# New slots for the side work of a two-stage attention kernel, and its second copy of the keys on ScalarE

## Chip, cores and metric

One NeuronCore of a Trainium2 chip runs the whole program. The metric is the time of one execution in microseconds (us), measured on the device; less is better. The kernel before takes 1200.07 us (median of 3 runs, 1199.62 to 1205.99).

## What is computed

The input is 16 images of 32 x 32 positions with 64 channels, float32. Cut to what matters, the reference is:

```python
# stage 1: group norm, then full attention over the 1024 positions of an image
h = group_norm(x, gn_scale, gn_bias, num_groups=16)
q, k, v = h @ wq + bq, h @ wk + bk, h @ wv + bv
w = softmax(q @ k.T * 64 ** -0.5)
t = x + (w @ v) @ wo + bo
# stage 2: layer norm over channels, then causal attention
n = layernorm(t)
q, k, v = n @ Wq.T, n @ Wk.T, n @ Wv.T
t = t + softmax(causal(q @ k.T / 8)) @ v
# stage 3: every one of 32 experts picks the top 8 positions of each image
u = layernorm(t)
p = softmax_over_positions(u @ gate_w.T + gate_b)
vals, idx = top_k(p, 8)                    # per image and expert
pooled = sum_k(vals * u[idx])              # one vector per image and expert
out = t + scatter_add(idx, vals * (gelu(pooled @ w1) @ w2))
```

## The kernel before

**The pipeline.** The attention part handles one image per iteration, 17 iterations in all (`emit(i)`; the first four and the last three written out, ten in a loop of two). Each iteration has two phases. Phase 1 of iteration i computes the scores and values of stage 1 for image i; phase 2 those of stage 2 for image i - 1. A phase is a list of units (`UNITS`): 16 units of 128 keys by 512 queries in phase 1, and 15 of 128 to 512 queries in phase 2, where the causal mask leaves some out. For each unit TensorE makes a score tile with two matmuls (`score`, L739 and L741: operands are split in a high and a low part, so two matmuls stand for one; the first also adds the row of negated maxima), ScalarE takes its exponential (`exponentials`, L883) into `probs`, and once for two key tiles TensorE multiplies with the values (`values`, L759; four groups per phase, the last of them run in the next phase). There are three score banks, so TensorE is at most three units ahead of ScalarE.

**Maxima first.** The exponential needs the maximum of each query's scores beforehand. So, one phase ahead, "pieces" compute the scores a first time (`piece`, L720), VectorE reduces each to a maximum (L1121), with two banks in turn (`NM` is 2). When the last piece is reduced, step `r1` or `r2` negates the maxima (L1111), transposes them on TensorE (L702), copies them out (L1116), and SP moves them by DMA (`move_row`, L584) into one row of `queries_lo`. The first score of the next phase waits for that DMA (`row_loaded`).

**Side work.** Everything else of an image is cut into named steps, each of which runs on several engines in turn: `p1.st`, `p1.g1`, `p1.g2`, `p1.g3`, `p1.w` (group norm statistics and the scaled weights), `p1.qa`, `p1.qb`, `p1.ka`, `p1.kb` (projections of queries and keys, two halves each: TensorE `mm`, ScalarE writes the high part `hi`, VectorE the low part `lo`), `xp` (splits the next input into high and low part), `f1.rs`, `f1.out`, `f2.out` (row sums and output projections), `l1a`, `l1b`, `l2a`, `l2b`, `l2c` (layer norms), `p2.tr`, `p2.qa`, `p2.qb` (transposition and projection for stage 2), `moe.tr`, `moe.lg` (gate logits), `r1`, `r2`. The steps of one chain (`proj_step`, `fin_step`, `norm_step`) count on one semaphore, so each waits for all before it in its chain.

**What sets the order.** Nothing is planned at run time. Each engine runs through the slots of a phase, two for each unit (32 in phase 1, 30 in phase 2). On TensorE an even slot begins with a score, then come value groups (`VALUE_SLOTS`; the last entry is a slot of the following phase), pieces (`PIECE_SLOTS`) and side steps (`AT["pe"]`). ScalarE does the exponential of the unit in its even slots, then `copy_out` (`COPY_SLOT`), then its side steps; VectorE its pieces, then its side steps; GpSimd the sums of the probabilities of stage 1 for the denominators (`add_rows`, L967 and L970, at `ADD_SLOTS`; the last in phase 2), the bias (`add_bias`, L977, at `BIAS_SLOT`), then its side steps. A slot is only a place in the order of one engine: an engine that has nothing to wait for goes on. The engines meet through semaphores. Steps in one slot follow the order of `SIDES_1` and `SIDES_2`. `AT_FIRST` replaces some entries in phase 1 of the first iteration.

**The second copy of the keys.** Stage 1 needs the high part of the keys twice: in `keys[1]` (its upper 64 partitions then receive the low part) and, with a row of ones, in `keys_hi`. The kernel before writes the first by ScalarE (L835) and has SP copy it to `keys_hi` by DMA (`copy_keys`, L576) once the low part of `p1.kb` is written. SP's order in an iteration is: load the transposed input of image i + 2 (`next_xt`), store image i - 2 (`store`), `copy_keys(i + 1)`, row 2 (`move_row(2, i - 1)`), load x of image i + 2 (`next_x`), row 1 (`move_row(1, i + 1)`). SP waits in this order too.

Of the kernel before, what the change touches and what calls it, by code (L numbers as in the profile page):

```python
# [18 lines left out]
HALF = S // 2  # L19
# [38 lines left out]
def sides_of(ph, first):  # L58
# [4 lines left out]
AT = {  # L63
# [9 lines left out]
}  # L73
AT_FIRST = {
    "pe": {"p1.g1": 1, "p1.g2": 2, "p1.w": 4},
    "act": {"p1.g1": 1, "p1.w": 4},
    "dve": {"p1.st": 0, "p1.g1": 1, "p1.g2": 2, "p1.g3": 3, "p1.w": 4},
    "pool": {"p1.g2": 2},
}

PIECE_SLOTS = {
    1: [1, 3, 5, 7, 9, 11, 12, 13, 14, 15, 16, 17, 19, 21, 23],
    2: [2, 3, 4, 6, 7, 8, 9, 10, 11, 12, 14, 16, 17, 19, 20, 22],
}
VALUE_SLOTS = {1: [9, 17, 25, 1], 2: [9, 17, 24, 1]}
ADD_SLOTS = [None, 4, 8, 12, 16, 20, 24, 1]
COPY_SLOT = {1: 2, 2: 2}
BIAS_SLOT = 6

# [83 lines left out]
def count_increments():  # L173
# [22 lines left out]
    inc("row_loaded1", ("row", 0), 16)  # L196
    inc("keys_copied", ("keys", 0), 16)
    for i in range(0, B + 1):
        for ph in (1, 2):
# [24 lines left out]
            if ph == 1 and i + 1 < B:  # L224
                inc("keys_copied", ("keys", i + 1), 16)
            if ph == 1 and 0 <= i - 2:
# [146 lines left out]
def attention_part(nc, ctx, g):  # L373
# [153 lines left out]
    def _(sp):  # L527
# [43 lines left out]

        def copy_keys(n):

            ready = held(done("proj_step", "p1.kb", n, "lo"))
            sp.wait_ge(proj_step, ready)
            sp.dma_start(keys_hi[n.parity][0:C, :].bitcast(F32), keys[1][n.parity][0:C, :].bitcast(F32)).then_inc(  # L576
                keys_copied, 16)

        def move_row(s, n):
# [15 lines left out]

        next_xt(Image(1))
        copy_keys(Image(0))
        move_row(1, Image(0))

        def emit(i):  # L600
            for k in range(IN_MAIN):
                if i.trip is None and (i.first == B - 1 and k < 2 or i.first == B and k == 2):
                    load_logits(k)
            if i.first + 2 < B:
                next_xt(i + 2)
            if i.first >= 2:
                store(i + (-2))
            if i.first + 1 < B:
                copy_keys(i + 1)
            if i.first >= 1:  # L610
                move_row(2, i + (-1))
            if i.first + 2 < B:
                next_x(i + 2)
            if i.first + 1 < B:
                move_row(1, i + 1)
# [195 lines left out]
    def _(act):  # L811
        def side(name, n):
# [18 lines left out]
            elif name in ("p1.qa", "p1.qb", "p1.ka", "p1.kb"):  # L831
# [3 lines left out]
                nc.scalar.activation(dst[:, a * HALF:(a + 1) * HALF], proj_ps[:, :], ACT.Identity,  # L835
                                     bias=qk_bias[q][:, b:b + 1], scale=1.0).then_inc(proj_step, 1)
            elif name == "p2.tr":
                act.wait_ge(proj_step, done("proj_step", name, n, "tr"))
# [540 lines left out]
```

## Time and profile before

| | before |
|---|---|
| median of 3 runs | 1200.07 us (1199.62 to 1205.99) |
| the profiled execution's own time | 1198.53 us |
| its span, first to last instruction | 1196.8 us |
| TensorE busy (matmuls) | 920.4 us, 77% of the span |
| VectorE busy | 586.5 us, 49% |
| ScalarE busy | 464.6 us, 39% |
| GpSimd busy | 418.9 us, 35% |
| mean granted TensorE clock | 0.845 |
| DMA, all queues | 47.53 MB, 40 GB/s over the span |

The busy time of an engine is the time in which an instruction of it runs. The granted clock is the share of full speed that TensorE was given; it has two levels, 1.2 and 2.4 GHz, so a mean of 0.5 is the lower level throughout. The attention part runs from about 50 to 1127 us; what follows is the expert part, which the change does not touch. In the rows further down, `[2.63 <-DMA queries_lo<-rows]` behind an instruction means that its engine stood idle 2.63 us before it and that the DMA named ended this.

### The profile page before, as it was taken

The numbers are of one execution on the slowest core, as the hardware profiler recorded it, in microseconds if no ns is written. First come the engines' busy times: TensorE is split into PE (matmuls) and PEld (weight loads), VectorE is DVE, ScalarE is ACT, GpSimd is POOL, SyncE is SP. The second block draws the span as 40 slices with busy tenths as digits, with TensorE's granted clock in tenths as the row PEclk, the third lists the DMA queues.
The fourth block names the chain that finished last, engine by engine and source line by source line (L and its number), as shares of the span: only waits on it lengthen the run. The fifth ranks groups of instructions, "written<-read, shape, count | busy, mean of one in ns | idle before, by whom it ended". The sixth has DMA issues, their size and how long they took to land. (4 is left out here: it accounts for less than half of the span.)

```text
span 1196.8 us, 14532 instructions
## 1 busy us (share of the span) xinstructions
PE 920.4 (77%) x4278; PEld 527.1 (44%) x4278; DVE 586.5 (49%) x1663; ACT 464.6 (39%) x952; POOL 418.9 (35%) x246
## 2 busy tenths in 40 slices
PE   2777888787888787887878887878878788866546
PEld 1334454534444453535444454545453444434326
DVE  3544554445564554544455544545454545544124
ACT  2222444353535343443435343434435353442320
POOL 1162524262616244242626152442426261610000
PEclk9985978798898888797988888897879888876758
DMA  4010011020201111010202011111102011000089
GB/s 89 11 43 27 18 27 36 5 58 9 58 10 45 23 27 40 27 40 1 57 9 57 9 45 22 26 40 27 31 9 57 9 31 36 23 18 23 18 177 268
DMA packets 67368, 47.53 MB, mean 40 GB/s; under 512 B 36047, under 2 KB 56815, under 8 KB 67311
## 3 DMA queue, kind: packets, MB, share of 16 engines
q1 hardware_dynamic: 67311, 46.90, 16.2%
q8 instruction: 20, 0.33, 0.1%
q14 instruction: 37, 0.30, 0.1%
HBM read 27.88 MB, written 10.49 MB: 32 GB/s over the span
## 5 line engine op out<-in xcount | busy, mean ns | idle before, releaser
L883 ACT ACTIVATE probs<-scores 128x512 f32<-128x512 f32 (+3 forms) x496 | 252.8, 514 | 455.9 <-PE scores L741 450.2
L1121 DVE TENSOR_REDUCE maxima<-maxima_in 128x1 f32<-128x512 f32 (+3 forms) x496 | 276.8, 581 | 271.9 <-PE maxima_in L720 268.0
L970 POOL TENSOR_TENSOR prob_sum<-prob_sum,probs 128x1024 f32<-128x1024 f32 x96 | 227.0, 2365 | 58.4 <-ACT probs L883 54.5
L720 PE MATMUL maxima_in<-keys,queries 128*128 128x512 f32 (+3 forms) x496 | 210.4, 453 | 27.8 <-DVE maxima L1121 27.3
L741 PE MATMUL scores<-queries,keys 128*128 128x512 f32 (+3 forms) x496 | 196.6, 397 | 0.0
L720 PEld LDWEIGHTS maxima_in<-keys,queries 128*128 128x128 f32 x496 | 108.7, 220 | 105.4 <-DVE maxima L1121 72.0
L739 PE MATMUL scores<-queries_lo,keys_hi 65*128 65x512 f32 x256 | 128.4, 502 | 34.2 <-DMA queries_lo<-rows 31.4
L759 PE MATMUL values_out<-probs,x_sb 128*64 128x512 f32 x512 | 144.7, 692 | 1.0 <-ACT probs L883 1.0
L937 POOL TENSOR_TENSOR ln<-ln,minus_half 128x8 f32<-128x8 f32 x32 | 52.8, 1649 | 251.5 <-DVE ln L1106 251.5
L947 POOL TENSOR_TENSOR x_stack<-x_twice,x_stack 64x1024 fp32r<-64x1024 f32 x16 | 37.4, 2339 | 229.9 <-ACT x_stack L819 229.9
L741 PEld LDWEIGHTS scores<-queries,keys 128*128 128x128 f32 x496 | 108.4, 218 | 8.2 <-issue 3.4
L739 PE MATMUL scores<-queries_lo,keys 128*128 128x384 f32 (+3 forms) x240 | 100.8, 420 | 0.0
L759 PE MATMUL values_out<-probs,normed 128*64 128x128 f32 (+3 forms) x480 | 99.5, 507 | 0.7 <-ACT probs L883 0.6
L967 POOL TENSOR_TENSOR prob_sum<-probs 128x1024 f32<-128x1024 f32 x16 | 37.8, 2364 | 150.0 <-ACT probs L883 119.4
L739 PEld LDWEIGHTS scores<-queries_lo,keys_hi 65*128 65x128 f32 x256 | 55.8, 218 | 58.0 <-issue 33.2
L739 PEld LDWEIGHTS scores<-queries_lo,keys 128*128 128x128 f32 x240 | 52.2, 217 | 36.0 <-issue 21.9
L759 PEld LDWEIGHTS values_out<-probs,x_sb 128*64 128x64 f32 x512 | 35.3, 155 | 72.5 <-issue 68.1
L737 PE MATMUL scores<-mask_k,ident_b 128*128 128x128 bf16 x128 | 31.8, 249 | 39.6 <-DMA queries_lo<-rows 39.6
L759 PEld LDWEIGHTS values_out<-probs,normed 128*64 128x64 f32 x480 | 34.6, 158 | 41.9 <-issue 37.2
L852 ACT ACTIVATE u_sb<-t,ln 128x64 f32<-128x64 f32 x128 | 45.5, 434 | 14.9 <-POOL ln L940 14.9
L737 PEld LDWEIGHTS scores<-mask_k,ident_b 128*128 128x128 bf16 x128 | 16.4, 128 | 54.5 <-DMA queries_lo<-rows 30.6
L719 PE MATMUL maxima_in<-mask_q,ident_b 128*128 128x128 bf16 x128 | 32.2, 252 | 7.5 <-DVE maxima L1121 6.7
(174 smaller groups left out, 1107.6 us busy)
## 6 DMA issues: line engine op xcount, KB each, us to landing
x_twice<-in_x_t SPq DMA_DIRECT2D x32, 256.0 KB, 4.1
x_halves<-in_x_t SPq DMA_DIRECT2D x16, 256.0 KB, 2.7
x_sb<-in_x SPq DMA_DIRECT2D x16, 256.0 KB, 3.0
keys_hi<-keys SPq DMA_DIRECT2D x16, 256.0 KB, 3.0
u_all<-u_sb SPq DMA_DIRECT2D x16, 256.0 KB, 2.6
t_scratch<-t SPq DMA_DIRECT2D x16, 256.0 KB, 3.0
total<-t_scratch SPq DMA_DIRECT2D x16, 256.0 KB, 4.9
w_sb<-in_w SPq DMA_DIRECT2D x1, 2080.0 KB
```

Source lines behind the costliest of these rows:

```text
L720: pe.matmul(maxima_in[:, p % NM, 0:w * P], queries[s][q][:, c * P:(c + 1) * P], keys[s][q][:, h * HALF:h * HALF + w * P], start=not diagon ...
L737: pe.matmul(bank[:, 0:P], ident_b[:, :], mask_k[:, :], start=True, stop=True)
L739: pe.matmul(bank, low[:, key_cols(t)], queries_lo[s][q][:, lo:hi], start=not diagonal, stop=False, skip_group_check=diagonal)
L741: pe.matmul(bank, keys[s][q][:, key_cols(t)], queries[s][q][:, lo:hi], start=False, stop=True, skip_group_check=diagonal).then_inc(scores_ ...
L759: mm = pe.matmul(values_out[a * C:(a + 1) * C, j0 * P:HALF], v_sb[:, t, :], probs[:, t % NP, lo:hi], start=t == 0, stop=t == NT - 1, skip_ ...
L852: ins = nc.scalar.activation(u_sb[:, t, :], t2[:, t, :], ACT.Identity, bias=ln[:, 2, t:t + 1], scale=ln[:, 1, t:t + 1])
L883: nc.scalar.activation(probs[:, t % NP, lo:hi], scores[:, (u + (s - 1) * len(UNITS_1)) % NST, 0:hi - lo], ACT.Exp, scale=SCALE).then_inc(e ...
L937: nc.gpsimd.tensor_tensor(ln[:, 1, :], ln[:, 0, :], minus_half[:, :], ALU.pow).then_inc(norm_step, 1)
L947: nc.gpsimd.tensor_tensor(x_stack[C:P, :], x_twice[C:P, :], x_stack[C:P, :], ALU.subtract).then_inc(split_step, 1)
L967: nc.gpsimd.tensor_tensor(prob_sum[:, :], probs[:, 0, :], new, ALU.add).then_inc(rows_added, 2)
L970: nc.gpsimd.tensor_tensor(prob_sum[:, :], prob_sum[:, :], new, ALU.add).then_inc(rows_added, 1)
L1121: V.reduce_max(maxima[s][:, c, h:h + 1], maxima_in[:, p % NM, 0:w * P], AX.X).then_inc(maxima_taken, 1)
```

## The change

All slot tables get new values, for TensorE (`pe`), ScalarE (`act`), VectorE (`dve`) and GpSimd (`pool`). `AT_FIRST` gets entries that hold the projections of the first iteration at their former slots. The DMA `copy_keys` and its wait leave SP's queue. In its place, ScalarE, after writing a half of the keys (`p1.ka`, `p1.kb`), waits for that write and copies the half from `keys[1]` to `keys_hi`; the semaphore `keys_copied` now counts 2 for an image instead of 16, and the first score of phase 1 waits for it as before.

```diff
 AT = {
-    "pe": {"f2.out": 2, "p1.qa": 6, "p1.qb": 11, "p1.ka": 16, "p1.kb": 22, "moe.tr": 24, "moe.lg": 26, "r2": 29,
-           "f1.rs": 3, "f1.out": 5, "p1.g1": 7, "p1.g2": 9, "p1.w": 12, "p2.tr": 15, "p2.qa": 19, "p2.qb": 22,
-           "r1": 26},
-    "act": {"p1.qa": 7, "p1.qb": 12, "l2b": 14, "p1.ka": 17, "l2c": 18, "p1.kb": 23, "moe.tr": 25, "moe.lg": 27,
-            "p1.g1": 8, "p1.w": 13, "p2.tr": 15, "p2.qa": 19, "p2.qb": 22, "xp": 24},
-    "dve": {"f2.out": 2, "l2a": 4, "p1.qa": 8, "p1.qb": 13, "p1.ka": 18, "p1.kb": 24, "r2": 28,
-            "p1.st": 1, "f1.rs": 3, "f1.out": 5, "l1a": 6, "p1.g1": 7, "p1.g2": 9, "p1.g3": 11, "p1.w": 13,
-            "p2.tr": 16, "p2.qa": 20, "p2.qb": 23, "r1": 25},
-    "pool": {"l2a": 6, "l1a": 7, "l1b": 8, "p1.g2": 10, "xp": 25},
+    "pe": {"f1.rs": 2, "f1.out": 4, "p1.g1": 1, "p1.g2": 3, "p1.w": 9, "p2.tr": 20, "p2.qa": 27, "p2.qb": 29,
+           "r1": 26, "p1.qa": 6, "p1.qb": 14, "p1.ka": 16, "p1.kb": 22, "r2": 27, "f2.out": 6, "moe.tr": 23,
+           "moe.lg": 24},
+    "act": {"p1.g1": 0, "p1.w": 9, "p2.tr": 20, "p2.qa": 27, "p2.qb": 29, "xp": 22, "p1.qa": 6, "p1.qb": 12,
+            "p1.ka": 16, "p1.kb": 18, "l2b": 17, "l2c": 17, "moe.tr": 18, "moe.lg": 23},
+    "dve": {"p1.st": 0, "f1.rs": 3, "f1.out": 9, "l1a": 9, "p1.g1": 1, "p1.g2": 3, "p1.g3": 6, "p1.w": 10,
+            "p2.tr": 21, "p2.qa": 22, "p2.qb": 29, "r1": 21, "p1.qa": 7, "p1.qb": 14, "p1.ka": 20, "p1.kb": 26,
+            "r2": 29, "f2.out": 0, "l2a": 8},
+    "pool": {"l1a": 20, "l1b": 29, "p1.g2": 11, "xp": 29, "l2a": 17},
 }
 AT_FIRST = {
-    "pe": {"p1.g1": 1, "p1.g2": 2, "p1.w": 4},
-    "act": {"p1.g1": 1, "p1.w": 4},
-    "dve": {"p1.st": 0, "p1.g1": 1, "p1.g2": 2, "p1.g3": 3, "p1.w": 4},
+    "pe": {"p1.g1": 1, "p1.g2": 2, "p1.w": 4, "p1.qa": 6, "p1.qb": 11, "p1.ka": 16, "p1.kb": 22},
+    "act": {"p1.g1": 1, "p1.w": 4, "p1.qa": 7, "p1.qb": 12, "p1.ka": 17, "p1.kb": 23},
+    "dve": {"p1.st": 0, "p1.g1": 1, "p1.g2": 2, "p1.g3": 3, "p1.w": 4, "p1.qa": 8, "p1.qb": 13, "p1.ka": 18,
+            "p1.kb": 24},
     "pool": {"p1.g2": 2},
 }
 PIECE_SLOTS = {
-    1: [1, 3, 5, 7, 9, 11, 12, 13, 14, 15, 16, 17, 19, 21, 23],
-    2: [2, 3, 4, 6, 7, 8, 9, 10, 11, 12, 14, 16, 17, 19, 20, 22],
+    1: [7, 7, 11, 15, 17, 17, 18, 19, 21, 21, 23, 23, 24, 24, 26],
+    2: [0, 0, 1, 2, 4, 11, 13, 14, 15, 17, 17, 18, 19, 20, 21, 21],
 }
-VALUE_SLOTS = {1: [9, 17, 25, 1], 2: [9, 17, 24, 1]}
-ADD_SLOTS = [None, 4, 8, 12, 16, 20, 24, 1]
-COPY_SLOT = {1: 2, 2: 2}
-BIAS_SLOT = 6
+VALUE_SLOTS = {1: [15, 27, 28, 1], 2: [10, 22, 29, 0]}
+ADD_SLOTS = [None, 10, 21, 22, 25, 27, 29, 11]
+COPY_SLOT = {1: 0, 2: 1}
+BIAS_SLOT = 12
...
-    inc("keys_copied", ("keys", 0), 16)
+    inc("keys_copied", ("keys", 0), 2)
...
-                inc("keys_copied", ("keys", i + 1), 16)
+                inc("keys_copied", ("keys", i + 1), 2)
...
-        def copy_keys(n):
-
-            ready = held(done("proj_step", "p1.kb", n, "lo"))
-            sp.wait_ge(proj_step, ready)
-            sp.dma_start(keys_hi[n.parity][0:C, :].bitcast(F32), keys[1][n.parity][0:C, :].bitcast(F32)).then_inc(
-                keys_copied, 16)
-
...
-        copy_keys(Image(0))
...
-            if i.first + 1 < B:
-                copy_keys(i + 1)
...
                 nc.scalar.activation(dst[:, a * HALF:(a + 1) * HALF], proj_ps[:, :], ACT.Identity,
                                      bias=qk_bias[q][:, b:b + 1], scale=1.0).then_inc(proj_step, 1)
+                if b:
+
+                    act.wait_ge(proj_step, done("proj_step", name, n, "hi"))
+                    nc.scalar.copy(keys_hi[q][0:C, a * HALF:(a + 1) * HALF],
+                                   keys[1][q][0:C, a * HALF:(a + 1) * HALF]).then_inc(keys_copied, 1)
```

## Rows read from the trace of the kernel before

**Rows 1.** The table by stretch, middle of the run: us, busy (count) per engine, clock, DMA.

```profile
core 0: us, PE busy (x) PEld busy (x) DVE busy (x) ACT busy (x) POOL busy (x), PEclk, DMA share, GB/s
108.22:1044.40 936.18, 761.95 (x3306) 432.42 (x3306) 481.65 (x1397) 397.15 (x810) 379.53 (x216) 0.86 0.12 30
165.35:1014.09 848.74, 688.16 (x2994) 391.11 (x2994) 438.53 (x1277) 359.53 (x737) 336.93 (x193) 0.86 0.12 30
```

**Rows 2.** The same table inside one image (625.25 to 691.60 us), same columns.

```profile
627.40:634.60 7.20, 6.08 (x20) 5.02 (x21) 3.79 (x24) 2.95 (x5) 0.78 (x1) 0.54 0.00 0
...
656.78:662.20 5.42, 5.42 (x13) 1.83 (x14) 0.00 (x0) 0.60 (x1) 0.50 (x1) 0.50 0.00 0
...
670.00:675.30 5.30, 2.57 (x11) 1.55 (x10) 3.99 (x12) 1.17 (x3) 4.22 (x4) 1.00 0.09 21
675.30:683.00 7.70, 7.27 (x27) 4.31 (x28) 3.93 (x8) 3.32 (x7) 0.00 (x0) 0.56 0.00 0
683.00:691.60 8.60, 5.32 (x33) 3.65 (x34) 4.31 (x8) 3.77 (x9) 2.34 (x1) 1.00 0.01 1
```

**Rows 3.** The waits of TensorE, 165.35 to 1014.09 us: total, times, longest.

```profile
PE scores L737 <- DMA queries_lo<-rows: 33.9, 13, 2.9
PE scores L739 <- DMA queries_lo<-rows: 29.2, 14, 2.4
PE proj_ps L644 <- DVE affine L1030: 20.0, 12, 1.7
...
PE fin_ps L702 <- DVE neg_max L1111: 15.7, 13, 1.3
PE fin_ps L688 <- ACT out_raw L891: 15.4, 13, 1.3
```

**Rows 4.** The timeline: start, duration, engine; a values group, a score, half of `l2b`/`l2c`.

```profile
642.14 1.94 PE L759 MATMUL values_out<-probs,x_sb 128*64 128x512 f32 x8
...
644.29 0.39 PE L739 MATMUL scores<-queries_lo,keys_hi 65*128 65x512 f32 x1
...
644.52 0.39 PE L741 MATMUL scores<-queries,keys 128*128 128x512 f32 x1
...
645.44 1.42 ACT L852 ACTIVATE u_sb<-t,ln 128x64 f32<-128x64 f32 x4
```

**Rows 5.** The timeline at the ends of both phases: SP's DMAs and the first scores.

```profile
623.39 0.69 SPq L584 DMA_DIRECT2D queries_lo<-rows  x1
625.25 0.50 PE L739 MATMUL scores<-queries_lo,keys_hi 65*128 65x512 f32 x1 [1.92 <-DMA queries_lo<-rows]
...
653.56 0.54 SPq L576 DMA_DIRECT2D keys_hi<-keys  x1
...
654.20 0.70 SPq L584 DMA_DIRECT2D queries_lo<-rows  x1
...
656.78 0.29 PE L737 MATMUL scores<-mask_k,ident_b 128*128 128x128 bf16 x1 [2.63 <-DMA queries_lo<-rows]
```

**Rows 6.** Groups by line and shape, whole run: busy us, mean ns of one.

```profile
L970 POOL TENSOR_TENSOR prob_sum<-prob_sum,probs 128x1024 f32<-128x1024 f32 x96 | 227.0, 2365 | 58.4 <-ACT probs L883 54.5
L1121 DVE TENSOR_REDUCE maxima<-maxima_in 128x1 f32<-128x512 f32 x304 | 202.5, 684 | 155.2 <-PE maxima_in L720 152.1
L883 ACT ACTIVATE probs<-scores 128x512 f32<-128x512 f32 x304 | 179.2, 596 | 376.9 <-PE scores L741 373.4 <-POOL prob_sum L970 2.5
...
L840 ACT CAST keys<-proj_ps 64x512 fp32r<-64x512 f32 x16 | 9.3, 579 | 0.0
```

**Rows 7.** The timeline of `f2.out` and `l2a` on VectorE, and GpSimd's first add.

```profile
630.66 0.18 DVE L1077 RECIPROCAL recip<-fin_ps 128x4 f32<-128x4 f32 x1 [3.50 <-PE values_out L688]
...
631.95 0.68 DVE L1093 TENSOR_TENSOR t<-t 128x512 f32<-128x512 f32 x1
...
633.83 2.36 POOL L967 TENSOR_TENSOR prob_sum<-probs 128x1024 f32<-128x1024 f32 x1 [8.43 <-ACT probs L883]
...
634.49 1.72 DVE L1105 TENSOR_SCALAR ln<-ln_mv 128x8 f32<-128x8 f32 x1
...
636.13 0.16 DVE L1106 TENSOR_SCALAR ln<-ln_mv 128x8 f32<-128x8 f32 x1
```

## The prediction

> **What bounds the kernel now.** No engine does. I read first the table by stretch. An image takes 848.74 / 13 = 65.3 us in the middle of the run [rows 1]; in that time TensorE is busy 688.16 / 13 = 52.9 us, VectorE 33.7, ScalarE 27.7 and GpSimd 25.9, at a granted clock of 0.86. TensorE is nearest to a bound, but it waits, and runs slowly after waiting. The same table inside one image shows that [rows 2]: three stretches of 7.20, 5.42 and 7.70 us stand at clocks of 0.54, 0.50 and 0.56, that is mostly at the lower level (1.2 GHz), and ahead of two of them stands a thin stretch, TensorE busy 2.57 of 5.30 us and 5.32 of 8.60; ahead of the third stands a wait for a DMA. Then I read who holds TensorE up [rows 3]: the two rows of maxima that come back by DMA before each phase's first score (33.9 / 13 = 2.61 us and 29.2 / 14 = 2.09 us), the `affine` column (1.67), `neg_max` (1.21) and `out_raw` (1.18). So each phase ends in a chain (maxima, `neg_max`, transpose, row, DMA) with nothing left to do beside it, and its start is paid twice: the wait, and then the low clock. The change is worth what it puts beside these waits.
>
> **What it gives, per image.**
> - *Row 2 (end of phase 1).* `r2` goes from TensorE slot 29 to 27 and now has score 14, values group 2 and score 15 behind it. A score is two matmuls 0.23 us apart, 0.46; a group of eight takes 1.94 [rows 4]. That is 2.9 us. The row needs 2.57 us from issue to its first user [rows 5], plus the cast on VectorE, some 0.3. The wait goes; next late would be exp 13, long done. `neg_max` is covered by group 1 (1.94), which stands ahead of `r2` in slot 27. Gain 2.61 + 1.21, and the stretch at 0.50 behind it, 5.42 x 0.5 = 2.71: **6.5**.
> - *Row 1 (end of phase 2).* `r1` stays at TensorE slot 26, but the two `p2.q` projections move behind it (27, 29), with score 14 and group 2: about 2.9 us with their own wait, against 1.86 for the row [rows 5]. `f2.out` moves from slot 2 to 6, two scores later, so that the copy of `out_raw` which it waits for is done. Gain 2.09 + 1.18, and 6.08 us of work at 0.54 (x 0.46 = 2.80): **6.1**.
> - *Group statistics.* `p1.g1` and `p1.g2` move to slots 1 and 3, and GpSimd's `p1.g2` now stands ahead of `l1a` and `l1b`, not behind them; `p1.w` at slot 9 should find `affine` ready. Gain 1.67 + 7.70 x 0.44 = 3.39: **5.1**.
>
> Together 17.7 us.
>
> **What comes back, per image.**
> - *The copy of the keys.* The DMA (16 of 256 KB) leaves SP. In the old order it was issued at 653.56, just ahead of row 2 at 654.20, which took 0.7 us longer than row 1 [rows 5]; with row 2 hidden that is worth 0. SP's wait for `p1.kb` ahead of row 2 goes too; it would have ended before the row's cast (VectorE slots 26 and 29): 0. ScalarE gets two 64x512 copies. No row has this copy from SBUF; the nearest, 64x512 from PSUM, takes 0.58 [rows 6], and I take that, plus 0.1 for the wait on its own last result (ends: 0 if ScalarE has time to spare, 1.4 if all is on the path). From slot 16 on ScalarE then has in a row `p1.ka`, the first copy, `l2b` and `l2c` (2 x 1.42 [rows 4]), exp 9, `moe.tr`, `p1.kb`, the second copy and exp 10, which score 13 waits for. With 0.60 for each exp and each activation of 128x512 that is 7.2 us. TensorE's way from slot 16 to 26 is about 6.0, set by VectorE's ten reduces of 128 to 512 columns and `p1.ka`'s `lo`. So score 13 waits **1.2**; with a DMA it would not, so this part of the change speaks against it.
> - *`p1.ka`* waits for `p1.qb`'s `lo`, which VectorE does behind all of `l2a`. From `f2.out`: its scaling with one piece 1.3 and `l2a` 4.3 less 1.55 [rows 7], two `lo` of about 0.75 and two more small pieces, together 6.4 us, while TensorE has 5.8 of work; with the hops **0.8** (0 to 2.4). The 1.55: `nm` (L1105) took 1.72 us and ended when GpSimd's add (633.83 to 636.19) did; its twin L1106 took 0.16 just behind. In the new order GpSimd should be done with add 1 and the bias by then and wait for `l2a` itself, so I take 0.17.
> - *`r1`* waits behind `p2.tr` on VectorE (slot 21: piece 15 and two subtractions of as many columns, 0.68 each, `neg_max` and hops, 2.6) while TensorE has 1.8 us: **0.8** (0 to 1.5).
> - *The clock.* Rows 2 show low stretches behind thin ones. The new order still has one: eleven pieces in phase 2 that VectorE paces at 0.68 us each [rows 6]. I leave one stretch of the three, **3.0** (0 to 9).
>
> Costing nothing: `f1.rs`, `f1.out`, `l1a`, the bias and the other side work change place on engines that wait anyway (GpSimd is idle 39 of 65 us [rows 1]); VectorE, standing at slot 0 for `f2.out`, has no piece before slot 7, where the first now comes. The first image keeps its projection slots. If GpSimd's slack goes, the price is the second case below.
>
> A page bears on `l2a`. The Trainium skill (SBUF — State Buffer, § Who interferes with whom) says that a VectorE instruction with two SBUF inputs, not only one in a two-port mode, is shut out for a whole GpSimd instruction that reads SBUF. By it the add that opens `l2a`, which may now fall beside GpSimd's bias, would be up to 0.9 us late, and the time 13 us more. No run here shows that case; in the old order this add had an idle GpSimd beside it.
>
> **The sum.** 17.7 - 5.8 = 11.9 us per image. The order repeats from 108.22 to 1044.40 us, 936.18 / 65.3 = 14.3 images [rows 1]; I count nothing for the ends. 14.3 x 11.9 = 170 us. From the profiled execution's own 1198.5 us (its span is 1196.8) that leaves 1028.5; the median of the runs lies 1.5 above that execution, so **1030 us**, an image at 53.4.
>
> **The rivals.**
> - *As forecast* (70%): from 965 (of what comes back only the copy's wait stays: 16.5 x 14.3 = 236) to about 1080.
> - *GpSimd's adds and the clock take half of it* (20%). `l2a` now stands ahead of adds 2 to 7, six of 2.37 us [rows 6], and `f1.rs` waits for the last, with VectorE's pieces from the fifth on queued behind it. By my count the last add ends 3.0 us into phase 2 and TensorE asks for it at 4.2: 1.2 us to spare. If it is 4 us late, 2.8 is lost, and with a second low stretch (3.0) 6.1 us per image is left: 87 us, 1113. For: the adds are packed behind exps 9 to 15, which come late. Against: GpSimd's sum.
> - *The gains come back as new waits* (4%): row 2 lands after score 15 all the same and the low clock stays; 1200. The copy alone may well show nothing, its DMA being hidden.
> - *Slower, by the clock* (6%). If stretches that VectorE paces are thin everywhere, TensorE may hold its lower level for most of the image. Its work at full level is 52.9 x 0.86 = 45.5 us; its idle time, 12.4, becomes 12.4 - 8.8 + 2.8 = 6.4 by the terms above. It turns slower where the mean granted clock of the middle falls under 45.5 / 58.9 = 0.77. At 0.75 an image takes 67.1 us: 1225. Against: the waits ahead of the low stretches are shorter or gone.
>
> The range holds the forecast and the second case: **965 to 1115 us**. Faster by over 0.5% (about what a measurement of this kernel can tell from no change) 90%, within 4%, slower 6%.
>
> **What would show it.** Right: waits for `queries_lo<-rows` under 0.5 us each, no clock near 0.5 at the start of either phase, L1105 near 0.17 us, an image of 52 to 56 us, score 13 and `p1.ka` waiting about 1 us, no `keys_hi<-keys` DMA and two ScalarE copies of about 0.6. Wrong: waits of `f1.rs` on `prob_sum` of some us (the second case), a mean clock under 0.8 (the last), or a wait I have not named of over 2 us per image.

## The result, and the profile after

The changed kernel takes **924.47 us** (median of 4 runs, 921.86 to 927.96), the kernel before, run beside it on the same chip, 1202.93. The ratio is 0.7687, with a 95% interval of 0.7647 to 0.7728: 278 us faster. The profiled execution took 927.96 us, with a span of 926.1. The forecast was 1030 us with a range of 965 to 1115, so the direction was right and the gain was larger than the range allowed.

The table by stretch of the changed kernel answers [rows 1] (the middle, the same 13 images) and [rows 2] (one image, here its two phases apart). Its columns: the stretch and its length, busy time of the engines, TensorE's granted clock, DMA share, GB/s. The last row is the thin stretch of eleven pieces in phase 2.

```profile
143.51:757.18 613.67, 594.49 (x2994) 334.18 (x2993) 422.08 (x1277) 372.27 (x763) 347.20 (x193) 1.00 0.14 35
...
380.17:403.96 23.79, 23.00 (x110) 12.62 (x108) 13.95 (x46) 17.38 (x34) 17.20 (x9) 1.00 0.24 61
403.96:427.47 23.51, 22.88 (x124) 13.04 (x123) 18.59 (x53) 11.35 (x25) 9.74 (x7) 1.00 0.05 12
...
415.50:423.00 7.50, 7.08 (x34) 4.16 (x35) 7.35 (x14) 3.79 (x9) 3.50 (x3) 1.00 0.00 1
```

An image takes 613.67 / 13 = 47.2 us, and 65.3 before: 18.1 less. TensorE's busy time per image goes from 52.9 to 594.49 / 13 = 45.7 us with the same work in it, and its idle time from 12.4 to 1.5. The first difference, 7.2, is the clock (0.86 before, 1.00 now), the second, 10.9, is waits. Of the 270.7 us by which the span is shorter, 235.1 lie in these 13 images (848.74 - 613.67); 21.8 lie ahead of them (165.35 - 143.51) and 13.8 behind.

Who holds TensorE up in the middle, first in the kernel before, whose five largest rows are [rows 3]; these are rows that the prediction did not use:

```profile
PE maxima_in L720 <- DVE maxima L1121: 17.7, 34, 0.9
...
PE proj_ps L630 <- DVE queries_lo L1059: 11.8, 13, 0.9
PE fin_ps L678 <- DVE recip L1065: 6.8, 13, 0.6
PE proj_ps L625 <- DVE bias_full L1041: 5.3, 12, 1.0
PE maxima_in L719 <- DVE maxima L1121: 5.0, 13, 0.4
```

The same view of the changed kernel, in full; score 13's two matmuls are L731 and L733 here (L739 and L741 before), the pieces L712 (L720 before):

```profile
PE scores L731 <- ACT probs L880: 6.2, 13, 0.5
PE fin_ps L617 <- ACT u_sb L849: 2.7, 13, 0.3
PE scores L731 <- DMA queries_lo<-rows: 0.3, 1, 0.3
```

All that is left is 9.2 us in 13 images, and before it was 160.8 (the ten largest rows). The waits for the row DMAs (but one of 0.3), `affine`, `neg_max`, `out_raw` and the pieces are gone. Of what was expected to come back, score 13's wait is there, 0.48 us an image on the matmul; on the weight loads the same wait stands larger:

```profile
PEld scores L731 <- ACT probs L880: 17.4, 14, 1.4
...
PEld fin_ps L694 <- DVE neg_max L1108: 13.8, 26, 0.8
```

The timeline of the changed kernel in one image answers [rows 5] and [rows 7]: `f2.out`/`l2a` on VectorE, the first of the two copies on ScalarE, score 13, row 2 and the first score of phase 2.

```profile
386.07 0.76 DVE L1090 TENSOR_TENSOR t<-t 128x512 f32<-128x512 f32 x1
386.24 1.73 POOL L974 TENSOR_TENSOR x_bias<-x_sb,bias_full 128x512 f32<-128x512 f32 x1
...
388.69 0.17 DVE L1102 TENSOR_SCALAR ln<-ln_mv 128x8 f32<-128x8 f32 x1
...
391.32 0.62 ACT L832 CAST keys_hi<-keys 64x512 fp32r<-64x512 f32 x1
...
397.73 0.50 PE L731 MATMUL scores<-queries_lo,keys_hi 65*128 65x512 f32 x1 [0.47 <-ACT probs L880]
...
401.45 0.72 SPq L579 DMA_DIRECT2D queries_lo<-rows  x1
401.51 1.94 PE L751 MATMUL values_out<-probs,x_sb 128*64 128x512 f32 x8
...
403.96 0.23 PE L729 MATMUL scores<-mask_k,ident_b 128*128 128x128 bf16 x1
```

Row 2 is issued at 401.45 and its first user starts at 403.96, 2.51 us later, as far apart as the 2.58 in [rows 5]; but values group 2 and score 15 now fill the time, and no wait is marked. `nm` (L1102) takes 0.17 us, where it took 1.72 in [rows 7].

### The profile page after: what moved, and what is told of

Read it like the earlier page. It is cut to its first block and busy times, and to the rows that moved or that the text cites. A ratio compares the mean times of both kernels' runs of the same rounds, so it can differ in the third digit from the quotient of the medians.

```text
span 926.1 us, 14558 instructions
## 1 busy us (share of the span) xinstructions
PE 815.0 (88%) x4278; PEld 467.7 (50%) x4278; DVE 569.6 (61%) x1663; ACT 479.5 (52%) x984; POOL 431.0 (47%) x246
## 5 line engine op out<-in xcount | busy, mean ns | idle before, releaser
L880 ACT ACTIVATE probs<-scores 128x512 f32<-128x512 f32 (+3 forms) x496 | 241.3, 512 | 208.9 <-PE scores L733 182.3
L712 PE MATMUL maxima_in<-keys,queries 128*128 128x512 f32 (+3 forms) x496 | 199.2, 434 | 17.3 <-DVE maxima L1118 9.0
L733 PE MATMUL scores<-queries,keys 128*128 128x512 f32 (+3 forms) x496 | 179.9, 365 | 0.0
L712 PEld LDWEIGHTS maxima_in<-keys,queries 128*128 128x128 f32 x496 | 94.6, 198 | 87.7 <-DVE maxima L1118 66.0
L751 PE MATMUL values_out<-probs,x_sb 128*64 128x512 f32 x512 | 124.0, 605 | 0.3 <-ACT probs L880 0.2
L731 PE MATMUL scores<-queries_lo,keys_hi 65*128 65x512 f32 x256 | 114.9, 449 | 9.4 <-ACT probs L880 6.4
L733 PEld LDWEIGHTS scores<-queries,keys 128*128 128x128 f32 x496 | 97.0, 196 | 6.7 <-issue 0.2
L731 PE MATMUL scores<-queries_lo,keys 128*128 128x384 f32 (+3 forms) x240 | 88.6, 373 | 0.0
L751 PE MATMUL values_out<-probs,normed 128*64 128x128 f32 (+3 forms) x480 | 83.7, 439 | 0.0
L964 POOL TENSOR_TENSOR prob_sum<-probs 128x1024 f32<-128x1024 f32 x16 | 38.3, 2392 | 81.5 <-PE values_out L680 54.6
L731 PEld LDWEIGHTS scores<-queries_lo,keys_hi 65*128 65x128 f32 x256 | 50.1, 196 | 46.1 <-issue 20.1
L731 PEld LDWEIGHTS scores<-queries_lo,keys 128*128 128x128 f32 x240 | 47.5, 198 | 2.1 <-issue 1.2
L1056 DVE TENSOR_TENSOR queries_lo<-proj_ps,queries 128x512 fp32r<-128x512 f32 x32 | 22.1, 692 | 42.1 <-ACT queries L842 42.1
L842 ACT CAST queries<-proj_ps 128x512 fp32r<-128x512 f32 x32 | 18.8, 587 | 38.0 <-PE proj_ps L623 38.0
L622 PE MATMUL proj_ps<-x_stack,w_lo 128*128 128x512 f32 x64 | 31.8, 497 | 7.5 <-DVE keys L1047 3.6
```

The source lines that it names most:

```text
L622: pe.matmul(proj_ps[:, :], lo, src[:, a * HALF:(a + 1) * HALF], start=True, stop=False)
L712: pe.matmul(maxima_in[:, p % NM, 0:w * P], queries[s][q][:, c * P:(c + 1) * P], keys[s][q][:, h * HALF:h * HALF + w * P], start=not diagon ...
L731: pe.matmul(bank, low[:, key_cols(t)], queries_lo[s][q][:, lo:hi], start=not diagonal, stop=False, skip_group_check=diagonal)
L733: pe.matmul(bank, keys[s][q][:, key_cols(t)], queries[s][q][:, lo:hi], start=False, stop=True, skip_group_check=diagonal).then_inc(scores_ ...
L751: mm = pe.matmul(values_out[a * C:(a + 1) * C, j0 * P:HALF], v_sb[:, t, :], probs[:, t % NP, lo:hi], start=t == 0, stop=t == NT - 1, skip_ ...
L880: nc.scalar.activation(probs[:, t % NP, lo:hi], scores[:, (u + (s - 1) * len(UNITS_1)) % NST, 0:hi - lo], ACT.Exp, scale=SCALE).then_inc(e ...
```

## The experiments

Two theories stood after the result. **The sum**: the gain is the sum of the places that the prediction named (row 2, row 1, group statistics), each worth its wait and the low clock behind it, whatever stands around it. **The whole**: the places depend on each other; a wait that is taken away at one place comes back at another unless the whole order fits, and the lesser moves, the pieces' slots above all, carry much of the gain. Four sets were run, each set's kernels on one chip beside the kernel before (1202.91, 1202.18, 1201.53, 1199.99 us). What an expectation calls A and B is what it says of them itself.

**The changed kernel again**, as the base of the first set.

> The changed kernel again, as the measure for the others of this set: 0.769 of the kernel before, about 924 us.

Measured 924.1 us (922.13 to 928.14), ratio 0.7687 (0.766 to 0.7715).

**The new slots with the old DMA copy.**

```diff
-                if b:
-                    act.wait_ge(proj_step, done("proj_step", name, n, "hi"))
-                    nc.scalar.copy(keys_hi[q][0:C, a * HALF:(a + 1) * HALF],
...
+        def copy_keys(n):
+            ready = held(done("proj_step", "p1.kb", n, "lo"))
+            sp.wait_ge(proj_step, ready)
+            sp.dma_start(keys_hi[n.parity][0:C, :].bitcast(F32), keys[1][n.parity][0:C, :].bitcast(F32)).then_inc(
...
             if i.first >= 2:
                 store(i + (-2))
+            if i.first + 1 < B:
+                copy_keys(i + 1)
```

> The new slots, with the second copy of the keys by SP's DMA as before. Theory A (TensorE is the bound now: an image takes 47.2 us of which it is busy 45.7, and it waits for the exponential of score 13 only 0.5 us): at most 0.5 x 14 = 7 us less than the changed kernel, and no more than 10 us more, since row 2 then leaves SP behind 256 KB and its 2.5 us of cover are just used up. Theory B (the prediction: the copies hold up score 13 by 1.2 us per image): 17 us less, about 907.

Measured **911.45 us** (909.61 to 914.98), ratio 0.7584 (0.7556 to 0.7611): 12.7 us under the changed kernel on the same chip, between the two theories (at most 7, and 17), and the fastest of the kernels that compute all of it. By the waits of 13 images, TensorE waits for one thing in its middle, once:

```profile
PE maxima_in L722 <- DVE maxima L1123: 0.2, 1, 0.2
```

and by the table by stretch the gain lies in phase 1, where ScalarE made the copies (23.79 in the changed kernel; phase 2 has 23.51 there):

```profile
327.61:350.41 22.80, 22.66 (x110) 12.72 (x110) 13.95 (x46) 16.22 (x32) 17.20 (x9) 1.00 0.30 76
350.41:373.81 23.40, 22.77 (x124) 13.22 (x123) 18.77 (x53) 11.35 (x25) 9.75 (x7) 1.00 0.05 12
```

12.7 / 14.3 images is 0.89 us each. Of the matmul waits, 9.0 us in 13 images (0.69 each) went with the copies: score 13's, and a smaller one for `u_sb`, which ScalarE writes behind the first copy. So the ScalarE copies cost what stands between their exps, as the prediction's step on them said; the new slots would have been better without them.

**The old slots with ScalarE's copy**: the same part alone, put into the kernel before.

```diff
-            if i.first + 1 < B:
-                copy_keys(i + 1)
...
+                if b:
+                    act.wait_ge(proj_step, done("proj_step", name, n, "hi"))
+                    nc.scalar.copy(keys_hi[q][0:C, a * HALF:(a + 1) * HALF],
```

> The old slots, with the copy by ScalarE alone. Theory A (row 2 is not hidden there, and lands 0.7 us earlier without the keys ahead of it; ScalarE has time): 0.7 x 14.3 = 10 us less than the kernel before, ratio 0.992. Theory B (the copy was hidden and stays so): ratio 1.000. Theory C (two more copies on ScalarE delay the exponentials): ratio 1.01 or more.

Measured 1188.7 us (1186.56 to 1189.96), ratio 0.9876 (0.9844 to 0.9909): 14 us faster, near Theory A. In the old order row 2 stood behind the copy on SP's queue and TensorE waited for it; over the same stretch as in [rows 3] (165.35 to 1014.09 us) the waits for it are now shorter (33.9 us for 13 there, 2.6 each; here 1.8 each).

```profile
PE scores L727 <- DMA queries_lo<-rows: 23.3, 13, 1.9
```

The same edit thus gains 14 us in the old order and loses 13 in the new one: what waits at that place decides (row 2 there, score 13 here), not the copy's own 0.62 us.

**Row 2 last**: only `r2`'s transpose goes from TensorE slot 27 to 31, so that nothing stands behind it.

```diff
-           "r1": 26, "p1.qa": 6, "p1.qb": 14, "p1.ka": 16, "p1.kb": 22, "r2": 27, "f2.out": 6, "moe.tr": 23,
+           "r1": 26, "p1.qa": 6, "p1.qb": 14, "p1.ka": 16, "p1.kb": 22, "r2": 31, "f2.out": 6, "moe.tr": 23,
```

> The changed kernel with step r2 on TensorE moved from slot 27 to 31, behind the last score, so that its transposition, cast and DMA (about 3.6 us) stand bare at the end of phase 1. Theory A (such a wait is paid twice, as the prediction has it: 3.6 us and then a stretch at the lower clock, 2.7 us): 6.3 x 14.3 = 90 us more, about 1014, and the granted clock near 0.5 at the start of phase 2. Theory B (one wait alone does not lower the clock where all else is dense): 51 us more, about 975, clock 1.00. Theory C (VectorE or ScalarE has slack to make it up): under 20 us more.

Measured 983.31 us (982.13 to 984.68), ratio 0.817 (0.8135 to 0.8205): 59 us slower, 4.1 an image: in time nearer to Theory B, but the clock did fall, as in A. The timeline shows the wait, back at 2.25 us, and the table by stretch of 2 us what follows: the granted clock is 0.87, 0.50, 0.77 and then 1.00 again.

```profile
329.09 0.23 PE L729 MATMUL scores<-mask_k,ident_b 128*128 128x128 bf16 x1 [2.25 <-DMA queries_lo<-rows]
```

```profile
328.00:330.00 2.00, 0.91 (x4) 0.78 (x5) 0.00 (x0) 0.00 (x0) 1.76 (x1) 0.87 0.01 2
330.00:332.00 2.00, 2.00 (x7) 0.68 (x7) 1.52 (x3) 0.60 (x1) 0.00 (x0) 0.50 0.00 0
332.00:334.00 2.00, 2.00 (x7) 0.53 (x4) 0.55 (x3) 0.11 (x1) 0.00 (x0) 0.77 0.00 0
334.00:336.00 2.00, 2.00 (x17) 1.15 (x16) 1.61 (x4) 1.25 (x3) 0.00 (x0) 1.00 0.00 0
```

By the busy time of each slice, the clock costs 2.00 x 0.50 + 2.00 x 0.23 + 0.91 x 0.13 = 1.6 us, the wait 2.25: 3.8 of the 4.1. The prediction's way of reckoning, a wait and a low clock behind it, is right for one place; it had put row 2 at 6.5 with `neg_max` (1.21) and a longer low stretch (2.71).

**`f2.out` early**, at TensorE slot 2 as it was before.

```diff
-           "r1": 26, "p1.qa": 6, "p1.qb": 14, "p1.ka": 16, "p1.kb": 22, "r2": 27, "f2.out": 6, "moe.tr": 23,
+           "r1": 26, "p1.qa": 6, "p1.qb": 14, "p1.ka": 16, "p1.kb": 22, "r2": 27, "f2.out": 2, "moe.tr": 23,
```

> The changed kernel with step f2.out on TensorE back from slot 6 to slot 2, where it waits for the copy of out_raw (1.2 us in the kernel before). Theory A (wait and low clock, as in the old order): 1.2 + 2.8 = 4 us per image, 57 us more. Theory B (the wait alone): 1.2 us per image, 17 us more, clock 1.00. Theory C: VectorE starts l2a earlier and gives it back: within 5 us.

Measured 942.19 us (937.89 to 945.03), ratio 0.7854 (0.7812 to 0.7896): 18 us slower, 1.3 an image, the size that Theory B gave, but not by its wait. `f2.out` doesn't wait for `out_raw` here, whose copy stands a slot earlier in the changed kernel (`COPY_SLOT`). Instead VectorE's add that opens `l2a` now starts about 1.1 us after GpSimd's first add of the image, and takes 1.88 us (the median of all 16 images; 0.68 without a GpSimd instruction beside it). All of `l2a` is late by that, and behind it TensorE's `p1.ka` waits for `p1.qb`'s `lo`, 0.8 us an image:

```profile
294.25 2.39 POOL L964 TENSOR_TENSOR prob_sum<-probs 128x1024 f32<-128x1024 f32 x1 [5.52 <-ACT probs L880]
295.31 1.88 DVE L1090 TENSOR_TENSOR t<-t 128x512 f32<-128x512 f32 x1
...
300.20 0.50 PE L622 MATMUL proj_ps<-x_stack,w_lo 128*128 128x512 f32 x1 [0.74 <-DVE queries_lo L1042]
```

The granted clock stays at 1.00 over the middle, where TensorE's longest wait is 0.8 us.

```profile
170.00:700.00 530.00, 505.25 (x2528) 281.31 (x2530) 372.56 (x1089) 314.72 (x647) 293.51 (x164) 1.00 0.15 36
```

**Late group statistics**: `p1.g2`, `p1.g3` and `p1.w` are moved back.

```diff
-"p1.w": 9
+"p1.w": 12
...
-"p1.g2": 3, "p1.g3": 6, "p1.w": 10
+"p1.g2": 3, "p1.g3": 11, "p1.w": 13
...
-    "pool": {"l1a": 20, "l1b": 29, "p1.g2": 11, "xp": 29, "l2a": 17},
+    "pool": {"l1a": 20, "l1b": 29, "p1.g2": 29, "xp": 29, "l2a": 17},
```

(The first pair is TensorE's; ScalarE's goes from 9 to 13, the second pair is VectorE's.)

> The changed kernel with GpSimd's p1.g2 behind l1a and l1b as in the old order, and what hangs on it moved back to the old slots (VectorE p1.g3 11 and p1.w 13, TensorE p1.w 12, ScalarE p1.w 13). Theory A (the prediction's third gain: 1.67 us of waiting and 3.4 us of low clock): 5.1 x 14.3 = 73 us more. Theory B (only the wait, or less where the pieces around it fill it): 10 to 25 us more, clock 1.00.

Measured 1019.71 us, ratio 0.8494 (0.8446 to 0.8541): 95 us slower, 6.7 an image, more than either theory said. One wait is back, 72.9 us for 16 images, about 4.8 in most of them, and behind it the clock falls to the lower level:

```profile
PE proj_ps L636 <- DVE affine L1027: 72.9, 16, 8.3
```

```profile
359.74 0.38 PE L636 MATMUL proj_ps<-affine,channel_consts 128*128 128x1 f32 x2 [4.77 <-DVE affine L1027]
```

```profile
360.00:366.00 6.00, 6.00 (x21) 4.37 (x20) 3.86 (x8) 2.06 (x5) 0.00 (x0) 0.50 0.00 0
```

In these 6 us TensorE is busy throughout, at a clock of 0.50. A late place for GpSimd's `p1.g2`, and for what hangs on it, costs more here than the old order's own wait for `affine` (1.67) did.

**Less work for TensorE**, in the changed kernel: each projection leaves out the first of its two matmuls, the one with the low part of the weights, 1.4 us an image.

```diff
-            pe.matmul(proj_ps[:, :], lo, src[:, a * HALF:(a + 1) * HALF], start=True, stop=False)
-            return pe.matmul(proj_ps[:, :], hi, src[:, a * HALF:(a + 1) * HALF], start=False, stop=True)
+            return pe.matmul(proj_ps[:, :], hi, src[:, a * HALF:(a + 1) * HALF], start=True, stop=True)
```

> The changed kernel without the first of the two matmuls of every projection (six of 128x512 per image are left out, 0.23 us each, so the low part of the weights is missing). Theory A (TensorE is the bound): 1.4 us per image, 20 us less, about 905. Theory B (VectorE and the chains between the engines are the bound, TensorE is only dense): under 5 us less.

Measured 920.98 us, ratio 0.7673 (0.7637 to 0.7709), against 0.7687 (0.766 to 0.7715) for the changed kernel: by the medians 3 us less for some 20 us of work (1.4 x 14.3) taken away, and the intervals overlap, so it may be none. This is Theory B. TensorE, though busy 97% of the middle at full clock, isn't the sole bound: other waits take the place of a part of what was left out, 16.0 us in 13 images where they were 9.2.

```profile
PE scores L730 <- ACT probs L879: 6.1, 13, 0.5
PE proj_ps L622 <- DVE queries_lo L1041: 4.4, 13, 0.4
PE fin_ps L617 <- ACT u_sb L848: 3.2, 13, 0.3
PE scores L730 <- DMA queries_lo<-rows: 2.3, 6, 0.8
```

**The same left out of the kernel before** (the same edit, at its L630).

> The same six matmuls per image left out of the kernel before. Theory A (there waits are the bound): 0 to 10 us less, ratio 0.992 to 1.000. Theory B (TensorE's work counts in full, at its lower clock in part): 20 to 30 us less, ratio 0.975 to 0.983.

Measured 1187.19 us (1183.95 to 1194.06), ratio 0.9877 (0.9827 to 0.9927): 15 us less, between the two theories and some three quarters of the 20 us (which is the price at full clock), though TensorE was idle 12.4 us an image. So much of what was left out stood on the path between the waits there; an engine that waits often can still be the path in between.

**The same left out of the new slots with the DMA copy.**

> The new slots with the DMA for the copy of the keys, and without the first of the two matmuls of every projection (six of 128x512 per image, 1.4 us, are left out). Theory A (with ScalarE's copies gone, nothing holds TensorE up, so it is the bound): 1.4 x 14 = 20 us less than with the DMA alone, about 891. Theory B (VectorE and the chains between the engines are as long as TensorE's own work): under 7 us less, 904 to 911.

Measured 904.77 us, ratio 0.754 (0.7505 to 0.7575): 6.7 us under the kernel with the DMA copy alone (5 by the ratios), as Theory B had it. Even with score 13's wait gone, a third of the work at most is what comes back. That would fit several chains within a few tenths of a microsecond of each other; which ones they are was not shown.

**The old piece slots in the new order.** All stays as changed, but the pieces go back to their old slots (the last, 22, to 21 so that it stays ahead of `r1`), and VectorE's `f2.out` from 0 to 6, behind its pieces.

```diff
-            "r2": 29, "f2.out": 0, "l2a": 8},
+            "r2": 29, "f2.out": 6, "l2a": 8},
...
-    1: [7, 7, 11, 15, 17, 17, 18, 19, 21, 21, 23, 23, 24, 24, 26],
-    2: [0, 0, 1, 2, 4, 11, 13, 14, 15, 17, 17, 18, 19, 20, 21, 21],
+    1: [1, 3, 5, 7, 9, 11, 12, 13, 14, 15, 16, 17, 19, 21, 23],
+    2: [2, 3, 4, 6, 7, 8, 9, 10, 11, 12, 14, 16, 17, 19, 20, 21],
```

> The changed kernel with the pieces (the first computation of the scores and its maxima) back at their old slots, but for the last (22 to 21), and VectorE's f2.out at slot 6 so that the first pieces can pass it. Theory A (the prediction, which priced no gain for the pieces' slots: they fill what the other steps leave): within 10 us of the changed kernel. Theory B (their places are a part of the gain that was left out: VectorE paces them, and in the old places they stand in front of l2a and of the group statistics): 20 to 60 us more.

Measured 1085.64 us (1077.92 to 1086.44), ratio 0.9019 (0.8977 to 0.9062): **161 us slower** than the changed kernel, more than half of its whole gain, and far beyond Theory B. (VectorE's `f2.out` had to move with the pieces, so the 161 us are of both.) An image takes 58.2 us here. In 600 us (10.3 images) TensorE waits 54.6 us for pieces, 5.3 an image:

```profile
PE maxima_in L712 <- DVE maxima L1118: 54.6, 63, 2.8
```

The timeline shows one of them. VectorE opens `l2a` at 336.16 and is through with it only after 338.80, with no piece in between; TensorE has stood still for 2.73 us when its own piece starts at 339.43.

```profile
336.16 0.79 DVE L1090 TENSOR_TENSOR t<-t 128x512 f32<-128x512 f32 x1
...
338.80 0.17 DVE L1102 TENSOR_SCALAR ln<-ln_mv 128x8 f32<-128x8 f32 x1
...
339.43 1.07 PE L712 MATMUL maxima_in<-keys,queries 128*128 128x384 f32 x2 [2.73 <-DVE maxima L1118]
```

The low clock behind it, 0.54 over 6 us, is in the table by stretch:

```profile
339.00:345.00 6.00, 5.57 (x14) 2.51 (x16) 2.76 (x7) 1.17 (x2) 5.03 (x4) 0.54 0.11 23
```

**The new piece slots in the old order**: only that table changes in the kernel before.

```diff
-    1: [1, 3, 5, 7, 9, 11, 12, 13, 14, 15, 16, 17, 19, 21, 23],
-    2: [2, 3, 4, 6, 7, 8, 9, 10, 11, 12, 14, 16, 17, 19, 20, 22],
+    1: [7, 7, 11, 15, 17, 17, 18, 19, 21, 21, 23, 23, 24, 24, 26],
+    2: [0, 0, 1, 2, 4, 11, 13, 14, 15, 17, 17, 18, 19, 20, 21, 21],
```

> The kernel before with the new slots of the pieces alone. Theory A (the pieces' slots are worth by themselves what the changed kernel lost without them, 161 us): 100 us less than before or better, ratio under 0.92. Theory B (they fit only the other new slots: in the old order the pieces at the end of phase 1 come later and lengthen the chain to row 2): within 30 us of the kernel before on either side, ratio 0.975 to 1.025.

Measured 1252.51 us (1241.94 to 1259.44), ratio 1.0418 (1.0346 to 1.0491): **52 us slower** than the kernel before, outside both theories. Over 165 to 1014 us (12.15 images of 69.9), the wait for `affine` is 3.3 us in each image (1.67 before), that for the pieces of L720 1.8 (17.7 / 13 = 1.36 before), and row 2 still waits 2.6, as before. Two waits are new, 1.0 and 0.8 an image: for `p1.qa`'s or `p1.qb`'s `lo` (L1045) and for ScalarE's part of the group statistics (`gn`). So it isn't the chain to row 2 that got longer, as Theory B had it, but the waits for the group statistics and the projections; how the pieces' places bring that about is not shown.

```profile
PE proj_ps L644 <- DVE affine L1030: 39.6, 12, 3.4
PE scores L737 <- DMA queries_lo<-rows: 31.8, 12, 3.0
...
PE maxima_in L720 <- DVE maxima L1121: 21.9, 39, 1.2
...
PE proj_ps L630 <- DVE queries_lo L1045: 12.1, 18, 0.9
...
PE proj_ps L640 <- ACT gn L822: 9.8, 12, 0.9
```

**The ends of the phases alone**, in the kernel before: `r2`, values group 2, the two `p2.q` projections and `f2.out` as the prediction's steps *Row 2* and *Row 1* have them; the pieces and the rest stay old.

```diff
-    "pe": {"f2.out": 2, "p1.qa": 6, "p1.qb": 11, "p1.ka": 16, "p1.kb": 22, "moe.tr": 24, "moe.lg": 26, "r2": 29,
-           "f1.rs": 3, "f1.out": 5, "p1.g1": 7, "p1.g2": 9, "p1.w": 12, "p2.tr": 15, "p2.qa": 19, "p2.qb": 22,
+    "pe": {"f2.out": 6, "p1.qa": 6, "p1.qb": 11, "p1.ka": 16, "p1.kb": 22, "moe.tr": 24, "moe.lg": 26, "r2": 27,
+           "f1.rs": 3, "f1.out": 5, "p1.g1": 7, "p1.g2": 9, "p1.w": 12, "p2.tr": 15, "p2.qa": 27, "p2.qb": 29,
...
-            "p2.tr": 16, "p2.qa": 20, "p2.qb": 23, "r1": 25},
+            "p2.tr": 16, "p2.qa": 26, "p2.qb": 29, "r1": 25},
...
-VALUE_SLOTS = {1: [9, 17, 25, 1], 2: [9, 17, 24, 1]}
+VALUE_SLOTS = {1: [9, 17, 28, 1], 2: [9, 17, 29, 1]}
```

(ScalarE's `p2.qa` and `p2.qb` go to 27 and 29 as well.)

> The kernel before with only the ends of the phases rearranged: r2 at 27 and values group 2 of stage 1 behind it, p2.qa and p2.qb and values group 2 of stage 2 behind r1, f2.out at 6; all else at the old slots. Theory A (the prediction's first two gains stand by themselves: 12.6 us per image, less about 1.2 because neg_max is not covered here): 150 to 180 us less, ratio 0.85 to 0.875. Theory B (a wait that goes there comes back at the next place that the old pieces and steps hold up): 20 to 90 us less, ratio 0.925 to 0.985.

Measured 1125.12 us (1119.09 to 1127.47), ratio 0.9372 (0.9329 to 0.9416): 75 us faster: Theory B. The row waits are gone, but in the 730 us from 170 to 900 (12.1 images of 60.3) TensorE waits 30.6 + 17.2 us for pieces, 4.0 an image where it was 1.75 before, 2.1 for `neg_max` where it was 1.21, and 0.8 for `ut`, which is new. Its idle time went from 12.4 to 10.2 us an image and its busy time from 52.9 to 50.1; the clock is 0.93.

```profile
PE maxima_in L720 <- DVE maxima L1121: 30.6, 43, 1.1
PE fin_ps L702 <- DVE neg_max L1111: 25.7, 24, 1.7
...
PE maxima_in L719 <- DVE maxima L1121: 17.2, 25, 1.1
PE fin_ps L698 <- ACT ut L857: 9.9, 12, 0.8
...
PE scores L737 <- DMA queries_lo<-rows: 0.2, 1, 0.2
```

**What the set says.** The new piece slots cost 52 us in the old order and gain 161 in the new one. No sum of terms, one for each place, can give both, so the theory of the sum falls: what one table is worth depends on the others. The tables of the values, of GpSimd's adds and of the copies out were not moved alone; what they are worth is not shown.

## Why the prediction was wrong

**What failed is the paragraph that costs and gains nothing, and the sum over places.** The prediction looked at five waits, 114.2 of the 160.8 us, and took the rest of TensorE's idle time, 3.6 us an image, over unchanged (12.4 - 8.8 + 2.8); the runs showed it gone. The piece slots, the largest table of the diff, appear there in one clause, that VectorE "has no piece before slot 7". By rows, the miss of about 100 us (1028.5 against 927.96) is made up, at 14.3 images, so:

| term, per image | forecast | measured | worth in the run |
|---|---|---|---|
| waits not named in the sum (pieces 1.75, `p2.q` 0.9, row sums 0.5, `p1.w` 0.4) | 3.6 stay | 0 | 51 us |
| waits that come back | 2.8 | at most 1.5 | 19 us |
| low clock that stays: busy time of TensorE (52.9 - 8.9 + 3.0 forecast) | 47.0 | 45.7 | 19 us |
| first and last image | 0 | | some 12 us, the rest (21.8 + 13.8 ahead and behind, less 1.3 x 18.1) |

The table is an account, not a cause; the cause is in the last three experiments. The two steps *Row 1* and *Row 2* come to 12.6 x 14.3 = 180 us (163 without `neg_max`, which that run didn't cover), and when they alone were done they gave 75. Of the 5.9 us of waits an image that they take out (the two rows and `out_raw`), 3.7 formed again on balance, chiefly at the pieces (2.2), `neg_max` (0.9) and `ut` (0.8); and of the 5.5 us of low clock that they were to save, 2.8 were saved. What the prediction priced at 0, the pieces, is what lets the priced gains stand: without their new slots 161 us are lost.

Point by point:
- *Row 2 and row 1*: right in mechanism. The row waits fell to 0.3 us in all, and putting `r2` last brings 2.25 us of wait and 1.6 us of clock back. Undone by itself, though, row 2 is worth 4.1 an image, not 6.5, since in the new order `neg_max` stays covered and the low stretch is shorter.
- *`f2.out` at slot 6*: its wait for `out_raw` is gone, but not by this move: with `f2.out` back at slot 2 it stays gone, since the copy stands earlier. The old slot costs 1.3 an image by another way (GpSimd's first add holds up `l2a`); that this is near the 1.18 of [rows 3] is luck.
- *Group statistics*: `affine`'s wait is gone, as expected. The experiment put the place at 6.7 an image, against 5.1, with a longer wait (4.8) than the old order's 1.67, so it does not measure the step.
- *The copy of the keys*: right. The two copies took 0.62 us each (0.58 was assumed), score 13 waits for exp 10 as told, and the DMA version is 0.89 us an image faster (1.2 was expected). Its removal from SP was rightly counted as 0 with row 2 hidden; in the old order, where row 2 isn't hidden, it is worth 14 us.
- *`p1.ka` and `r1`*, 0.8 us each: neither is on TensorE's matmuls. The first came where `f2.out` was early (0.74 in the line shown); the second stands only on the weight loads (13.8 us for 26, those of `r2` among them, 0.5 each). `nm` at 0.17 us was right.
- *The clock*: the 3.0 us an image that were to stay low are not there. The miss is only 1.3, because the other side was too large as well: the three low stretches were priced at 2.71 + 2.80 + 3.39 = 8.9 (the last by the length of its stretch, 7.70, not TensorE's 7.27 busy in it), and all the clock gave back was 7.2. That the two partly cancel is luck. The one thin stretch that was feared, eleven pieces that VectorE paces, ran with TensorE busy 7.08 of 7.50 us at 1.00: VectorE's 0.68 us a piece leaves TensorE the scores, so it isn't thin.
- *The second rival*, GpSimd late: it did not happen. In one image the last of GpSimd's adds started at 404.92 and was through at 407.28; `f1.rs` on TensorE (L660) started at 408.32, 1.0 us later (1.2 to spare was the forecast), and no wait for it is marked. *The third rival*, row 2 still late: one wait of 0.3 in 13 images. *The fourth rival*, the clock: the middle's mean is 1.00.

The timeline of the changed kernel for that place:

```profile
404.92 2.36 POOL L967 TENSOR_TENSOR prob_sum<-prob_sum,probs 128x1024 f32<-128x1024 f32 x1 [0.42 <-ACT probs L880]
...
408.32 0.64 PE L660 MATMUL fin_ps<-prob_sum,ones_f 128*32 128x256 f32 x8
```

**The add that opens `l2a`.** In [rows 7] the add of VectorE with two SBUF inputs took 0.68 us, beside an idle GpSimd. In the changed kernel it starts at 386.07 and takes 0.76, and GpSimd's bias starts at 386.24 beside it and takes 1.73. The instructions of that line in the changed kernel, with the least, median and largest duration in ns; in the kernel before the median was 1.28 us:

```profile
L974 POOL TENSOR_TENSOR x_bias<-x_sb,bias_full x16: 1276/1734/1787, 59.3 to 763.2; 128x512 f32<-128x512 f32 x16
```

The two shortest of these, 1.276 and 1.277, are the two images in which no such VectorE add runs beside it. The prediction had the add late by up to 0.9 us (no row gives this number), and it lost 0.08. The Trainium skill (SBUF — State Buffer, § SBUF: two separate sides) says that of a VectorE instruction with two SBUF inputs and a GpSimd instruction that reads SBUF, the one that starts first has the shared ports for its whole instruction and the other is held. The trace agrees, with VectorE first here and GpSimd held by 0.45 us, on an engine with slack. The other order is in the run with `f2.out` early: there GpSimd's first add starts about 1.1 us ahead, and VectorE's takes 1.88 us and ends 0.55 after it, in thirteen images within 0.01 us. So the 13 us that the prediction worked out from the page did not come in the changed kernel, where VectorE's add starts only 0.2 us before that GpSimd add is through; a loss of that kind came where `f2.out` was early (1.2 us an image, and the run 18 us slower).

## What to carry to other kernels

Price a reordering as a whole: take the list of all the waits on the nearest engine, small ones too, and ask of each where its releaser stands in the new order, since a wait that is taken out at one place can form again at the next one that isn't moved along (75 us gained where the two places alone promised 163 or more). An engine that is busy 97% of the time at full clock isn't by that the sole bound: taking out 20 us of its work gave about 3. When an experiment gives the number that a theory forecast, look whether the wait that it named is the one that came back: `f2.out` early cost what was expected by another way. The best order here is the new slots with the copy left to the DMA, 911 us: nothing waits for that transfer there, while ScalarE has a chain to keep.

## What the runs showed of the hardware

- The clock fell behind the longer waits and not behind the short ones. After a wait of 2.25 us (row 2 last) the granted clock was 0.50 to 0.77 for 4 us, after one of 2.73 (old pieces) 0.54 over 6, after one of 4.77 (late statistics) 0.50 over 6; where `f2.out` was early, with no wait over 0.8 us in the middle, it stayed at 1.00.
- The same stall reads differently on matmuls and on weight loads: score 13 waits 0.48 us an image on TensorE's matmuls and 1.24 on its weight loads, and when the copies were taken off ScalarE 0.89 came back (0.69 of it from matmul waits, `u_sb`'s among them).
- GpSimd's 128x512 add of two SBUF tiles took a median of 1.28 us in the kernel before and 1.73 here, beside a VectorE add with two SBUF inputs that had started 0.17 us earlier; VectorE's took 0.76 against 0.68. Behind GpSimd's 128x1024 add, started about 1.1 us ahead, the same VectorE add took 1.88.
- The 128x8 `nm` on VectorE took 0.17 us in every image here (171 to 172 ns) where it took a median of 1.63 and up to 1.74 before; in [rows 7] it ended with the GpSimd add that had started ahead of it.
